# A macaron block on one core: the first phase reordered, the first attention's buffers cleared there, its start and its tail rearranged

## The reference

```python
x = x + 0.5 * _L0_ffn_ref(_layernorm(x), router_w, expert_bias, w1, w3, w2, sw1, sw3, sw2)   # F0a
x = x + _L0_attn_ref(_layernorm(x), ...)      # A0: 16 heads of 8, band of |i - j| <= half
x = x + 0.5 * _L0_ffn_ref(_layernorm(x), ...) # F0b
x = x + 0.5 * _L1_ffn_ref(_layernorm(x), ...) # F1a: top 2 of 8 experts with a capacity
x = x + _L1_attn_ref(_layernorm(x), ...)      # A1
x = x + 0.5 * _L1_ffn_ref(_layernorm(x), ...) # F1b
```

## Time and profile before

| | |
|---|---|
| median of 3 runs (all) | 3185.7 us (3185.64, 3185.7, 3187.7) |
| the profiled execution's own time | 3189.26 us |
| its span, first to last instruction | 3187.5 us |
| busy: PE, DVE, ACT, POOL | 2611.3, 2328.8, 2261.4, 1904.3 us |
| mean granted TensorE clock | 0.854 |
| P | 0 to 51 us |
| F0a | 51 to 427.6 us |
| A0 | 427.6 to 867.6 us |

### The profile page before, as it was taken

The page is one execution under the profiler, slowest core; times in us unless marked ns, Lnnn a source line. Parts: engine busy times, 40 slices in busy tenths (PEclk is TensorE's granted clock), DMA queues, the critical chain, the costliest instruction groups (busy, mean ns, idle before and its releaser), DMA issues. The chain is left out here.

```text
span 3187.5 us, 42265 instructions
## 1 busy us (share of the span) xinstructions
PE 2611.3 (82%) x12174; PEld 1734.8 (54%) x12208; DVE 2328.8 (73%) x4338; ACT 2261.4 (71%) x2559; POOL 1904.3 (60%) x1486
## 2 busy tenths in 40 slices
PE   4999958999789996799985778777787787469998
PEld 3877745555478774678872223232232232158887
DVE  5677746666466675898877687787787878378887
ACT  2555526777545554577764999999999999557776
POOL 2766667777456675444444666666766767344444
PEclk9999979999899998899996666676767666679999
DMA  3111100000011111111100000000000000111111
GB/s 114 54 40 53 39 1 1 2 1 1 1 55 54 53 39 66 55 54 40 45 21 1 0 0 1 1 1 1 1 1 1 1 1 1 53 51 44 53 39 53
DMA packets 13588, 86.72 MB, mean 27 GB/s; under 512 B 2176, under 2 KB 4224, under 8 KB 4224
## 3 DMA queue, kind: packets, MB, share of 16 engines
q1 hardware_dynamic: 13440, 84.96, 7.2%
HBM read 82.33 MB, written 2.62 MB: 27 GB/s over the span
## 5 line engine op out<-in xcount | busy, mean ns | idle before, releaser
L1743 POOL TENSOR_TENSOR A_Y<-A_Y,A_U 128x2048 f32<-128x2048 f32 x86 | 389.9, 4555 | 226.8 <-ACT A_U L1786 226.8
L1819 DVE TENSOR_SCALAR A_U<-ps 128x1024 f32<-128x1024 f32 x256 | 309.3, 1219 | 126.1 <-POOL A_Y L1743 62.4
L1825 DVE SCALAR_TENSOR_TENSOR A_U<-ps,A_U 128x1024 f32<-128x1024 f32 x256 | 311.4, 1216 | 58.2 <-PE ps L1955 58.2
L1955 PE MATMUL ps<-A_QT,A_KT 9*128 9x512 f32 x512 | 181.4, 705 | 195.8 <-DVE A_U L1825 163.3
L477 POOL TENSOR_TENSOR F0b_h<-F0b_h,dn 128x512 f32<-128x512 f32 x128 | 211.9, 1660 | 123.7 <-DVE F0b_h L408 123.5
L477 POOL TENSOR_TENSOR F0a_h<-F0a_h,dn 128x512 f32<-128x512 f32 x128 | 212.0, 1661 | 117.4 <-DVE F0a_h L408 117.2
L513 POOL TENSOR_TENSOR gated<-half_neg 128x1 f32<-128x1 f32 x179 | 37.7, 210 | 397.8 <-ACT F1a_h L359 178.3
L1743 POOL TENSOR_TENSOR dn<-dn,A_U 128x2048 f32<-128x2048 f32 x42 | 190.2, 4553 | 112.6 <-ACT A_U L1786 112.6
L1955 PEld LDWEIGHTS ps<-A_QT,A_KT 9*128 9x128 f32 x512 | 66.0, 254 | 335.5 <-DVE A_U L1825 238.4
L1265 DVE CUSTOM_DVE_ANT_0 ps<-ps,A_mask 128x256 f32<-128x256 f32 (+1 forms) x512 | 185.1, 423 | 84.4 <-PE ps L1335 78.8
L1786 ACT ACTIVATE A_U<-A_U 128x2048 f32<-128x2048 f32 (+1 forms) x96 | 236.5, 2464 | 0.0
(11 more groups left out here) (365 smaller groups left out, 8366.6 us busy)
## 6 DMA issues: line engine op xcount, KB each, us to landing
dn<-weight_rows SPq DMA_DIRECT2D x32, 1024.0 KB, 4.7
F1a_cwb<-weight_rows SPq DMA_DIRECT2D x16, 1024.0 KB, 4.7
F1b_cwb<-weight_rows SPq DMA_DIRECT2D x16, 1024.0 KB, 4.7
dn<-in_down SPq DMA_DIRECT2D x2, 2048.0 KB, 12.1
stage<-in_up SPq DMA_DIRECT2D x1, 2560.0 KB, 9.4
X<-in_x SPq DMA_DIRECT2D x1, 2048.0 KB, 8.4
F1a_h<-in_up SPq DMA_DIRECT2D x1, 2048.0 KB, 7.5
F1b_h<-in_up SPq DMA_DIRECT2D x1, 2048.0 KB, 7.7
```

The lines of the kernel that those rows point to most:

```text
L1743: eng.tensor_tensor(flat(y_slot(m, h)), flat(y_slot(m, h)), flat(Um[:, h % UR]), ALU.add).then_inc(s["t_ready"], 1)
L1819: eng.tensor_scalar(u_step(n), d_pair(n), 0.0, None, ALU.max).then_inc(s["dp_vector"], 1)
L1825: eng.scalar_tensor_tensor(out=u, in0=g_pair(), scalar=CLAMP, in1=u, op0=ALU.min, op1=ALU.mult).then_inc(s["u_ready"], 1)
L1955: last = eng.matmul(ps[:, 4 + b, :], KT[r:r + 9, pair, kt * P:(kt + 1) * P], QT[r:r + 9, pair, :], start=True, stop=True)
```

## The change

In P, `x` comes in four transfers with a semaphore each, followed by the router weights, `up0`, `down0` and three more on SP; the other small transfers and the 16 of `wo_t` are issued by ScalarE. VectorE computes the statistics of chunk c + 1 and then applies the norm of chunk c. ScalarE rounds a quarter of `up0` after each second chunk, and VectorE subtracts by quarters. `QA`, `KA`, `VA`, the mask and `own` get memory that lives from P to F0b, GpSimd clears the first three at the end of P, and VectorE makes the mask's distances there. In A0 only `QZ` is cleared, keys are projected, taken, written and transposed ahead of queries, the mask follows behind both, `kz_ready` is given after two of four instructions, and at the end the four tiles go through four banks.

```diff
-                    eng.dma_start(X[:, :, :], x).then_inc(load["x"], 16)
-                    for dst, src in ((rw[0], router0), (rw[1], router1), (wfc, wfc0), (qkv_w[0], w_qkv0),
-                                     (qkv_w[1], w_qkv1), (out_w[1], wo1)):
-                        eng.dma_start(dst[:, :], src).then_inc(load["small"], 16)
...
-                    eng.wait_ge(consts_ready, 1)
-                    for h in range(H):
-                        eng.dma_start(wo_t[...], wo0_t[h]).then_inc(load["small"], 16)
+                    for i in range(PARTS):
+                        tiles = slice(i * TILES // PARTS, (i + 1) * TILES // PARTS)
+                        eng.dma_start(X[:, tiles, :], x[:, tiles, :]).then_inc(x_in[i], 16)
+                    eng.dma_start(rw[0][:, :], router0).then_inc(load["router"], 16)
                     eng.dma_start(stage[:, :], up0).then_inc(load["up0"], 16)
                     eng.dma_start(dn0[:, :, :, :], down0).then_inc(load["rest"], 16)
+                    for dst, src in ((qkv_w[0], w_qkv0), (qkv_w[1], w_qkv1), (out_w[1], wo1)):
+                        eng.dma_start(dst[:, :], src).then_inc(load["small"], 16)
@@ gpsimd, P, behind the last power
+                    eng.memset(A0_QA[...].bitcast(F32), 0.0)
+                    eng.memset(A0_KA[...].bitcast(F32), 0.0)
+                    eng.memset(A0_VA[...], 0.0)
+                    eng.drain()
+                    eng.memset(A0_VA[:, :, :, HD:HD + 1], 1.0)
+                    eng.memset(A0_KA[:, :, :, 3 * HD:3 * HD + 1].bitcast(F32), 1.0)
+                    eng.drain()
@@ scalar, P: 8 small transfers, wait consts_ready 1, 16 of wo_t, then
                     for c in range(B):
                         eng.wait_ge(s["tr_done"], c + 1)
                         eng.activation(XT[...], ps[:, c % 6, :], ACT.Copy).then_inc(s["xt_copied"], 1)
+                        if c % 2:
+                            if c == 1:
+                                eng.wait_ge(load["up0"], 16)
+                            cols = slice(c // 2 * part, (c // 2 + 1) * part)
+                            eng.activation(up0_hi[...][:, cols], stage[:, cols], ACT.Copy).then_inc(s["split_done"], 1)
@@ vector, P
+                    stats(0)
                     for c in range(B):
+                        if c + 1 < B:
+                            stats(c + 1)
                         eng.wait_ge(s["rstd_ready"], c + 1)
                         for i in range(TPC * c, TPC * (c + 1)):
                             last = eng.tensor_scalar(xn_0[:, i, :], X[:, i, :], mv_0[:, i, 0:1], rstd_0[:, i:i + 1],
                                                      ALU.subtract, ALU.mult)
                         last.then_inc(s["xn_ready"], 1)
+                    eng.wait_ge(consts_ready, 2)
+                    eng.tensor_reduce(A0_own[...], ident[...], AX.X, ALU.add)
+                    eng.tensor_copy(dist[:, 0, :], dist_i[:, :])
+                    eng.scalar_tensor_tensor(out=dist[:, 1, :], in0=dist[:, 0, :], scalar=-1.0, in1=dist[:, 0, :], ...)
+                    eng.tensor_scalar(A0_mask[:, :], dist[:, 1, :], 2.0, None, ALU.mult)
+                    for i in range(PARTS):
+                        eng.wait_ge(s["split_done"], i + 1)
+                        eng.tensor_tensor(up0_lo[...][:, cols], stage[:, cols], up0_hi[...][:, cols], ALU.subtract)
@@ A0: GpSimd clears QZ alone, then rows_k(0), rows_q(0, 0), spread(0, 0); in spread
                             for j in range(4):
                                 last = eng.tensor_scalar(KZ[:, g % 2, j, :], ...)
-                            last.then_inc(s["kz_ready"], 1)
+                                if j % 2:
+                                    last.then_inc(s["kz_ready"], 1)
@@ A0, vector: the mask steps stand in mask_of_columns
-                        take_q(0)
                         take_k(0)
+                        take_q(0)
+                        mask_of_columns()
@@ A0, tensor: in scores and at the start
+                                if t == 0:
+                                    eng.wait_ge(s["kz_ready"], 2 * (TPC * c + g) + i + 1)
-                        project(0)
-                        eng.wait_ge(s["qs_ready"], 1)
-                        project(1)
-                        eng.wait_ge(step, n0 + 5)
-                        eng.wait_ge(s["asm_done"], 2)
+                        project(1)
+                        eng.wait_ge(s["qs_ready"], 1)
+                        project(0)
+                        eng.wait_ge(s["asm_done"], 1)
                         turn(0, KA, 0)
+                        eng.wait_ge(s["asm_done"], 2)
                         turn(1, QA[:, 0], 0)
@@ A0, tensor: the tail (vector divides from bank t into rden_4[:, t])
+                        eng.wait_ge(s["m_ready"], B * HALVES)
+                        eng.wait_ge(s["taken"], 3 + TURNED * B)
+                        eng.wait_ge(s["ot_copied"], TPC * B)
                         for t in range(TPC):
-                            turn_out(eng, B, t)
+                            for g in range(4):
+                                last = eng.transpose(ps[:, t, g * P:(g + 1) * P], OT[:, g, t * P:(t + 1) * P], ident[:, :])
+                            last.then_inc(s["on_tr"], 1)
```

More of the change, by code:

```diff
@@ L71, in macaron @@
         col = sb("col", [P, 24])
-        load = {k: sem(f"load_{k}") for k in ("x", "up0", "up1", "rest", "small", "dn1")}
+        load = {k: sem(f"load_{k}") for k in ("router", "up0", "up1", "rest", "small", "dn1")}
         up1_top, up1_split = sem("up1_top"), sem("up1_split")
@@ L729, in macaron @@
             iota_i = sb("iota_i", [P, E], I32, st)
+            dist_i = sb("dist_i", [P, WIN], I32, st)
+            dist = sb("dist", [P, 2, WIN], F32, st)
+            PARTS = 4
+            x_in = [sem(f"x_in{i}") for i in range(PARTS)]
             def body(block):
@@ L789, in _ @@
                         if c == 1:
-                            eng.wait_ge(load["small"], 16 * (12 + H))
+                            eng.wait_ge(load["router"], 16)
                         if c > 0:
@@ L797, in _ @@
                     last.then_inc(s["lg_done"], 1)
+                    eng.wait_ge(load["small"], 16 * (11 + H))
                     eng.matmul(ps[:, 6, 0:D], wo_t[:, :], wfc[:, :], start=True, stop=True).then_inc(step, 1)
@@ L803, in _ @@
                 def _(eng):
+                    eng.dma_start(ebias[:, 0, :], expert_bias.to_broadcast([P, E])).then_inc(load["small"], 16)
+                    eng.dma_start(rw[1][:, :], router1).then_inc(load["small"], 16)
+                    eng.dma_start(wfc[:, :], wfc0).then_inc(load["small"], 16)
+                    eng.dma_start(alpha_s[:, :], alpha.to_broadcast([P, 1])).then_inc(load["small"], 16)
+                    for n, dst in enumerate((bq_s, bk, bv, bfc)):
+                        eng.dma_start(dst[:, :], bias_rows0[n:n + 1, :].to_broadcast([P, D])).then_inc(load["small"], 16)
+                    eng.wait_ge(consts_ready, 1)
+                    for h in range(H):
+                        eng.dma_start(wo_t[h * HD:(h + 1) * HD, h * HD:(h + 1) * HD], wo0_t[h]).then_inc(load["small"], 16)
+                    part = U0 * 2 * HID0 // PARTS
                     for c in range(B):
@@ L816, in _, with stats @@
                 def _(eng):
-                    eng.wait_ge(load["x"], 16)
-                    for c in range(B):
+                    def stats(c):
+                        if c % (B // PARTS) == 0:
+                            eng.wait_ge(x_in[c * PARTS // B], 16)
                         tiles = range(TPC * c, TPC * (c + 1))
@@ L970, in attn0 @@
                 rden = ab("rden", [P, H])
+                rden_4 = ab("rden_4", [P, TPC, H])
                 on, oT = xn, xT_c
@@ L979, in attn0 @@
                     s, lay, lambda t, g: OT[:, g, t * P:(t + 1) * P], on, oT, rden[:, :], SPARE)
[L980 to L983, removed]
+                mask = A0_mask
+                own = A0_own
                 mask_b = ab("mask_b", [P, 2 * WIN], BF16)
@@ L1155, in chunk @@
                                     else:
+                                        if first and g == 1:
+                                            eng.wait_ge(pad_ready, 1)
                                         take_shifted(number, QZ[:, (g + 3) % 2])
@@ L1244, in take_k @@
                         def take_k(k):
-                            eng.wait_ge(s["pj_done"], 3 * k + 2)
-                            if not (isinstance(k, int) and k == 0):
+                            if isinstance(k, int) and k == 0:
+                                eng.wait_ge(s["pj_done"], 1)
+                            else:
+                                eng.wait_ge(s["pj_done"], 3 * k + 2)
                                 eng.wait_ge(s["asm_done"], 2 * k)
@@ L1342, in shifted @@
                             n = UNITS * c + u
+                            if isinstance(n, int) and n == 0:
```

(1 more changed line is left out.)

109 lines of the change are left out of this document (55 added, 54 removed).

## The result

| | before | after |
|---|---|---|
| median (lowest to highest) of 7 runs | 3186.59 us (3185.09 to 3187.71) | 3175.76 us (3174.3 to 3178.44) |
| ratio, 95% interval | | 0.9966 (0.9955 to 0.9977) |
| profiled execution's span | 3187.5 us | 3176.6 us |
| granted clock, mean | 0.854 | 0.853 |

The kernel became faster, by 10.8 us. The forecast was 23.5 us and 3162.2 us; the time lies outside its range, above 3172. So the question is where half of the gain went. Every block ends in a barrier, so the lengths of the blocks tell which has the loss (all in us, each from its profiled execution). P, F0a, A0 and F0b start with the first instruction behind the barrier. F1a and F1b are counted from GpSimd's first rounding of `xs` (L230), some 20 us behind theirs, so that F0b and A1 hold 20 us that belong to the next block: from barrier to barrier F0b takes 384.8 us before and 390.0 after.

The account below looks back on a forecast made before the run. It took P as a serial chain, A0's start as waiting on GpSimd and its tail as a ladder through one bank. 10.2 + 10.5 + 2.8 = 23.5 us off 3185.7 gives 3162.2 us, range 3153 to 3172.

Parts of the forecast that it names:

- the sum: Whole kernel: P 10.2, A0's start 10.5 and its tail 2.8 us give 23.5 us, 3162.2 us for the median.
- rival 4: TensorE-bound work: shifted bursts change when its clock is granted, kernel slower by 6.4 us or more; chance 0.03.
- What would show it: Signs: bn_stats at 5.1, F0a's first instruction near 41, A0 427 us long, F0b to F1b unchanged within 1 us.
- if a later block changes its length: Blocks behind the change: a sign that the prediction is wrong, with no size given.
- P: Block P: ends at 40.2 instead of 50.44 us with the clears fully holding the norm, worth 10.2 us.
- rival 2: P's input: four parts share the way with ScalarE's small transfers, land near 9.2; 4.1 us less, 3166.3 us; chance 0.12.
- The holding: End of P: GpSimd's clears keep VectorE's norm of the last chunk waiting for their full length, 6.6 us.
- rival 1: End of P: the clears hold nothing, P ends at 33.6 and the time is 3155.6 us; chance 0.25.
- A0's start: Start of A0: first spread ends 9.2 us earlier, chunk 0 gains 10.2, later chunks 0.3; worth 10.5 us.
- The halves: A0's copies: first half announced early saves about 0.6 and 0.4 us in chunk 0, 0.3 in later chunks.
- The tail: End of A0: four banks cut first transpose to the one back from 6.1 to 3.3 us, worth 2.8 us.
- 3: A0's start: gain given back, something other than GpSimd holds chunk 0; worth 5 or less, 3168 to 3172 us; chance 0.07.

Follow-up runs that it names:

- Experiment 1: Kernel before with 32 unused bytes behind dn0: 3199.7 us, ratio 1.0039; also the changed kernel with A0_own padded to 64 bytes: 3172.57 us.
- e12: Changed kernel with A0_own padded to 1,024 bytes and nothing else: 3164.38 us, ratio 0.9929.
- experiment 2: Changed kernel with GpSimd's clears moved, QA ahead of the first power, KA and VA in quarters behind the first four: 3169.95 us, ratio 0.9949.
- experiment 3: Changed kernel with x loaded in one transfer instead of four: 3179.46 us, P 45.1 us against 41.5.
- e8: Kernel before with 32 unused bytes ahead of dn_hi, so that only dn_hi and dn_lo move: 3196.54 us, F0a 380.9 us.
- e10: Changed kernel with ScalarE holding back its transfers until the first part of x has landed: 3176.94 us, P 41.2 us.

## Why the prediction was wrong

**The step that failed** is the sum itself: it has P and the two edges of A0, and puts F0a and F0b at nothing. The reason given is rival 4's "the change leaves F0a and the middle as dense as they are", and "What would show it" says "F0b to F1b should keep their lengths within 1 us". F0a grew by 6.3 and F0b by 5.2 us. The step had been read as one about the clock and about waits, and both were right: from 200 to 300 us the granted clock was 1.00 and PE waited for nothing. What was not weighed at all is that memory which is added in one phase moves the buffers of the next. The 32 bytes by which the added buffers miss a multiple of 256 cost 11.5 us. Experiment 1 shows it with the kernel before alone, and e12 gives 11.4 us back (3175.76 - 3164.38) with nothing but padding. The prediction did name the sign, "if a later block changes its length", but no cause or price for it.

**P** was forecast at -10.2 and is -9.5. The start came at 6.37 instead of 5.1, by ScalarE's small transfers (4.74 without them): the sharing that rival 2 named is real and costs 1.6 us, which the sum had left out. The holding, which made the difference between the forecast and rival 1, was 6.1 instead of 6.6 us. The parts were worth 3.6 us with this start against 4.1. VectorE's small steps (33.10 to 34.41) took 1.3 for 1.4, the four subtractions 5.69 for 5.49.

**A0's start** was forecast at 10.5. The first masked copies came 8.8 us earlier in the block (forecast 9.2): the mask's comparison, which took 0.79 us, and its copies ran beside GpSimd's casts, and GpSimd stood idle 0.45 us before its subtraction at 436.98. That these make up the missing 0.4 is argued, not tested. The halves gave 1.1 us where 0.6 + 0.4 were put down to chunk 0 and 0.3 to later chunks; the last 0.3 did not show. Together 9.9.

**The tail** was forecast at 2.8. The ladder gave 6.11 - 2.93 = 3.2, and from the transpose back to the block's end it is 12.28 us (837.74 to 850.02) instead of 13.59 (854.03 to 867.62), another 1.3. As much is the clock: that transpose became shorter by 0.5 and the projection by 0.9 us, at a granted clock of 1.00 (834 to 841 us, 2.4 GHz) where it was 0.50 before (852 to 860 us, 1.2 GHz). Together 4.5, so that A0 as a whole came 1 us better than forecast. That is luck: the sum had no term for the clock in the tail. No run takes back the order of keys, queries and mask or the tail by itself; their shares are read from the timelines.

**The rivals.** 1 (nothing held) fell with experiment 2, 2 with experiment 3, 3 with A0's 14.3 us. Rival 4 was the only one to weigh a loss in work that the change does not touch. It looked for it in the clock, at the price of 40 us at half speed, and took F0a to be safe; what came is matmuls 2.3% slower in two blocks at full speed. The time lies outside the range because none of its cases had a block that pays without a changed line.

**What stays open.** The runs show that the pace hangs on how the start addresses of the FFN's buffers and its weights' stand to each other modulo 256 bytes: at 32, 64 and 128 bytes off the pace is 230 to 232 ns and at 0 it is 227. They don't show why, nor which accesses meet: e8 slowed matmuls whose own two buffers had not moved. Distances between 128 and 256 were not tried, nor any that are no multiple of 32.

## What to carry to other kernels

When a change allocates or frees on-chip memory, the blocks that follow get other addresses: compare the length of each block, and the mean of TensorE's groups, also where no line is changed, and in this kernel keep the buffers that its matmuls read congruent modulo 256 bytes. Large clears belong beside bn_stats, loads or matmuls, and not beside VectorE's norms or small additions: moving them within the same phase gave 6 us. A signal given at half of a batch of copies is worth something only while the reader waits for them, here at the first two groups of the first chunk.

## What the runs showed of the hardware

- The start-to-start time of 128x512 matmuls at a granted clock of 1.00 was 227.2 ns with all operand buffers congruent modulo 256 bytes and 230.1 to 232.4 ns with one or more of them 32, 64 or 128 bytes off. Each pair of lines has its own narrow value then, from 224.5 ns (L269 to L270) to 235.1 (L251 to L252) in the changed kernel.
- ScalarE issued the 16 transfers of `wo_t` in 5.98 us in the changed kernel and in 10.27 us when it began late (e10), where SP took 5.43 us for these 16; its 8 other small transfers took 0.39 to 0.79 us each. With them under way beside it, the first part of `x` came 1.6 us later.
- VectorE's norm under GpSimd's clears was stopped for 6.1 of 7.3 us, while bn_stats beside a clear were not slowed at all (0.86 us). A 128x4 addition was: 0.80 us instead of 0.17.
